# Summing four bilinear corners by one strided VectorE reduce in place of two adds

## The chip, the cores and the metric

One core of a Trainium2 chip. The metric is the device time of one execution in microseconds, the median of several runs.

## The reference

Four images of 128 channels and 56 x 56 pixels, float32. A 1x1 convolution to 32 channels (with batch norm and relu) gives h; a 3x3 convolution of h gives, per pixel, 18 offsets and 9 masks. Then comes a deformable convolution: at each of nine taps h is sampled bilinearly at a shifted position, weighted, and contracted.

```
def gather(yi, xi):
    valid = (yi >= 0) & (yi < Hi) & (xi >= 0) & (xi < Wi)
    ...
    return out * valid[:, None].astype(img.dtype)
return gather(y0, x0) * (wy0 * wx0)[:, None] + gather(y0, x0 + 1) * (wy0 * wx1)[:, None] \
     + gather(y0 + 1, x0) * (wy1 * wx0)[:, None] + gather(y0 + 1, x0 + 1) * (wy1 * wx1)[:, None]
...
samp = _bilinear(h, y, x) * mask[:, None]
out = jnp.einsum('bckhw,ock->bohw', samp, w2.reshape(w2.shape[0], w2.shape[1], 9))
```

A 1x1 convolution back to 128 channels, batch norm, the residual x and relu close the first block. The second is self-attention over the 3136 pixels of an image: f and g of 16 channels give the logits, a softmax over the keys weights h (16 channels), and its projection to 128 channels, times gamma, is added to the input.

## The kernel before

**Front.** For each image TensorE makes h in four shifted copies, VectorE and ScalarE evacuate them, and a table in HBM is written in which one row of 128 floats (512 bytes) holds a pixel's four bilinear corners, 32 channels each. The 27 offset and mask channels go through HBM too.

**Groups and tiles.** The 12544 pixels are taken in 14 groups of 896; a group is 7 tiles of 128 pixels, one pixel per partition (98 tiles). For each group VectorE works out the row indices `IDX` and the corner weights `CW` (`index_step`), two groups ahead in the later part.

**Gathers.** GpSimd (POOL) issues for each tile nine indirect DMAs (L477), one per tap, each fetching a row of 4 x 32 floats per partition into `G[:, j, ...]`, with a memset of a scratch tile `pad` (L484) between two of them. `G` has one slot for each of a group's 7 tiles, so the gathers of tile j of group g wait until VectorE has finished with tile j of group g - 1 (the semaphore `s_s2` before the change). There are 882 gathers and 784 memsets.

**A tile on VectorE.** In a slot the order is tap, corner, channel: 9 x 4 x 32 = 1152 floats. `tile_mul` multiplies them in place by the weights in two instructions (20 and 16 blocks of 32, L1038); `tile_pairs` (L1045) adds corners 0 and 2 to corners 1 and 3 into `S2`, 576 results, both inputs in SBUF; `tile_sum` (L1052) adds the halves of `S2` into `S`, 288 results. TensorE transposes `S` (L578), ScalarE copies it to `ST`, TensorE contracts it with w2 (L586), ScalarE writes `h2`.

**Attention.** A planner (`plan`) writes out a list of ticks for TensorE, VectorE and ScalarE. A tick has a logits block of 112 queries by 448 keys (`logits1`, L602, into PSUM banks L1a and L1b), whose row maximum VectorE takes (`reduce1`, L1060), a second logits block with queries and keys exchanged (L619), its exp on ScalarE (L812), and every fourth tick the product with the values (`weigh`, L633). `l1_free` makes a logits block wait for the reduce two blocks earlier. After a pass over keys come small steps for maxima and sums; `cut` (L1094) splits f and g into bfloat16 parts, with two inputs in SBUF. L1131 and L1174 add the attention and the first block's result to X.

**Order.** `half(g, h, ...)` runs through 28 steps i. HALVES says at which i a tile starts: {3: 0, 7: 1, 13: 2, 19: 3} in the first half, {4: 4, 11: 5, 17: 6} in the second. On VectorE the first product comes at i, the second at i + 1, the pair add at i + 2, the sum at i + 3; TensorE's `tile_in` comes at i + 5. Each step ends with the planned ticks, on all three engines in the same order, 22 to 36 in a half. Groups 0 to 3 run among the fronts of the images. After the last group a half without tiles and the rest of the ticks follow.

Of the kernel before, what the change touches and what calls it, by code (L numbers as in the profile page):

```python
# [27 lines left out]
ALU = mybir.AluOpType  # L28
ACT = mybir.ActivationFunctionType
AX = mybir.AxisListType  # L30

IMAGES, C, HW = 4, 128, 56
CB = 32
# [6 lines left out]
TPG = GROUP // 128  # L40
TAPS = 9
# [27 lines left out]
HALVES = [{3: 0, 7: 1, 13: 2, 19: 3}, {4: 4, 11: 5, 17: 6}]  # L69
# [4 lines left out]
FIN_LAST = dict(w3=0, residual=0, relu=0, project=1, project_in=1, project_g=1, g_in=2, ht_out=3,  # L74
                ht_in=3, cast1=3, cut1=4, cast2=6, cut2=7)
OFFSETS, INDEX, MASKS = 20, 21, 22
TILE_PAIRS, TILE_SUM = 2, 3
TILE_IN, TILE_OUT, TILE_H2 = 5, 7, 7
NEXT = 16
ROWS = 11  # L80
# [151 lines left out]
def build(nc, xt, params, coords, out):  # L232
# [3 lines left out]
    with ExitStack() as ctx:  # L236
        def sb(name, shape, dt=F32):
            return ctx.enter_context(nc.sbuf_tensor(name, shape, dt))
# [4 lines left out]
        def sem(name):  # L243
            return ctx.enter_context(nc.semaphore(name))
# [19 lines left out]
        CW = sb("CW", [128, IRING, TPG, 36])  # L264
        IDX = sb("IDX", [128, IRING, TPG, TAPS], I32)
        G = sb("G", [128, TPG, TAPS * 4 * CB])
        S2 = sb("S2", [128, TAPS, 2 * CB])
        S = sb("S", [128, 2, TAPS * CB])
        ST = sb("ST", [96, 2, 384])
        h2 = sb("h2", [CB, GROUP])  # L270
# [49 lines left out]
        s_it, s_im = sem("s_it"), sem("s_im")  # L320
        s_ie, s_ix = sem("s_ie"), sem("s_ix")
        gathered = [sem(f"gathered{j}") for j in range(TPG)]
        s_mul, s_s2, s_sum = sem("s_mul"), sem("s_s2"), sem("s_sum")
        s_pt, s_st, s_w2 = sem("s_pt"), sem("s_st"), sem("s_w2")
        s_h2 = sem("s_h2")
        s_w3, s_xs, s_x = sem("s_w3"), sem("s_xs"), sem("s_x")
# [33 lines left out]
        def span(h, i):  # L360

            if not FIRST_HALF <= h <= LAST_HALF:
                return range(0)
            lo, n = bound[h], (BLOCKS if h == LAST_HALF else bound[h + 1] - bound[h])
            return range(lo + i * n // BLOCKS, lo + (i + 1) * n // BLOCKS)
# [5 lines left out]
        def after(eng, sem_, count):  # L371


            if not isinstance(count, int) or count > 0:
                eng.wait_ge(sem_, count)
# [88 lines left out]
        @block.gpsimd  # L464
        def _(eng):
            eng.memset(H4[:, :], 0.0).then_inc(s_zero, 1)
            eng.memset(HT[:, :, CI:CI + 1], 1.0).then_inc(s_zero, 1)
            eng.wait_ge(s_zero, 2)
            eng.memset(G6[96:99, :], 1.0).then_inc(s_zero, 1)
            eng.wait_ge(s_zero, 3)  # L470

            def gather(g, images):
                eng.wait_ge(s_ix, NEXT * g + ROWS)
                for j in range(TPG):
                    after(eng, s_s2, TPG * (g - 1) + j + 1)
                    for k in range(TAPS):
                        eng.indirect_dma_start(  # L477
                            G[:, j, k * 4 * CB:(k + 1) * 4 * CB], None,
                            table[0:images * POS, :],
                            bass.IndirectOffsetOnAxis(ap=IDX[:, g % IRING, j, k:k + 1], axis=0))\  # L480
                            .then_inc(gathered[j], 16)
                        if k < TAPS - 1:
                            after(eng, s_pad, (TPG * g + j) * (TAPS - 1) + k)
                            eng.memset(pad[:, :], 0.0).then_inc(s_pad, 1)  # L484

            def tables(n):
                eng.wait_ge(tab_dma[0], 16 * 4 * n)
                eng.wait_ge(tab_dma[1], 16 * 3 * n)

            tables(1)  # L490
            for g in range(3):
                gather(g, 1)
            tables(IMAGES)
            for g in range(3, GROUPS):
                gather(g, IMAGES)
# [434 lines left out]
        def _(eng):  # L930
# [99 lines left out]
            def tile_mul(g, j, first):  # L1030

                eng.wait_ge(gathered[j], 16 * TAPS * (g + 1))
                eng.wait_ge(s_ix, NEXT * (g + 1))
                rows = G[:, j, 0:20 * CB] if first else G[:, j, 20 * CB:]
                n = 20 if first else 16
                weights = CW[:, g % IRING, j, 0:20] if first else CW[:, g % IRING, j, 20:36]
                rows = rows.rearrange("p (k c) -> p k c", c=CB)
                eng.tensor_tensor(rows, rows, weights.unsqueeze(2)  # L1038
                                  .to_broadcast([128, n, CB]), ALU.mult).then_inc(s_mul, 1)

            def tile_pairs(g, j):
                n = TPG * g + j
                eng.wait_ge(s_mul, 2 * (n + 1))
                pair = G[:, j, :].rearrange("p (k a c) -> p k a c", k=TAPS, a=2)
                eng.tensor_tensor(S2[:, :, :], pair[:, :, 0, :], pair[:, :, 1, :], ALU.add)\  # L1045
                   .then_inc(s_s2, 1)

            def tile_sum(g, j):
                n = TPG * g + j
                eng.wait_ge(s_s2, n + 1)  # L1050
                after(eng, s_pt, n - 1 if j else n)
                eng.tensor_tensor(S[:, j % 2, :].rearrange("p (k c) -> p k c", c=CB),  # L1052
                                  S2[:, :, 0:CB], S2[:, :, CB:2 * CB], ALU.add).then_inc(s_sum, 1)

            def reduce1(x):

# [30 lines left out]
            def cut(fin, side, first):  # L1087

                cut_ = P("cut_g" if side else "cut_f", STACK)
                k = 0 if first else 1  # L1090
                to = FG[0:STACK, side, :] if first else \
                    (G6 if side else F6)[0:STACK, bass.ds(fin * CHUNK, CHUNK)]
                eng.wait_ge(s_c1 if first else s_c2, 2 * fin + 1 + side)
                eng.scalar_tensor_tensor(  # L1094
                    out=to, in0=FGh[:, side, :], scalar=cut_[:, k:k + 1],
                    in1=FG[0:STACK, side, :], op0=ALU.mult, op1=ALU.add)\
                    .then_inc(s_d1 if first else s_cut, 1)
# [58 lines left out]
            def half(g, h, fin, idx=None):  # L1156

                at = FIN_LAST if g is None else FIN
                for i in range(BLOCKS):
                    if g is not None and i in HALVES[h]:  # L1160
                        tile_mul(g, HALVES[h][i], True)
                    if g is not None and i - 1 in HALVES[h]:
                        tile_mul(g, HALVES[h][i - 1], False)
                    if g is not None and i - TILE_PAIRS in HALVES[h]:
                        tile_pairs(g, HALVES[h][i - TILE_PAIRS])
                    if g is not None and i - TILE_SUM in HALVES[h]:
                        tile_sum(g, HALVES[h][i - TILE_SUM])
                    for k in range(3 * (i - INDEX), 3 * (i - INDEX) + 3):
                        if idx is not None and 0 <= k < NEXT:
                            index_step(idx, k)  # L1170
                    if fin is not None and i == at["residual"]:
                        eng.wait_ge(s_w3, fin + 1)
                        xc = X[:, fin * CHUNK:(fin + 1) * CHUNK]
                        eng.scalar_tensor_tensor(out=xc, in0=M[:, 0:CHUNK], scalar=scale[:, 2:3],  # L1174
                                                 in1=xc, op0=ALU.mult, op1=ALU.add)\
                            .then_inc(s_xs, 1)
                    if fin is not None and i == at["ht_in"]:
                        eng.wait_ge(s_hT, fin + 1)
                        eng.tensor_copy(HT[:, 4 * fin:4 * fin + 4, 0:CI],
                                        M[0:KT, 0:4 * CI].rearrange("p (k c) -> p k c", c=CI))\  # L1180
                           .then_inc(s_ht, 1)
                    if fin is not None and i in (at["cut1"], at["cut1"] + 1):
                        cut(fin, i - at["cut1"], True)
                    if fin is not None and i in (at["cut2"], at["cut2"] + 1):
                        cut(fin, i - at["cut2"], False)
                    for t in span(LAST_HALF if g is None else 2 * g + h, i):
                        attend(t)
# [22 lines left out]
            front(1)  # L1210
            next_indices(2)
            half(0, 0, None)
            half(0, 1, 0)
            for b in range(2, IMAGES):
                front(b)
                next_indices(b + 1)
                half(b - 1, 0, 2 * b - 3)
                half(b - 1, 1, 2 * b - 2)
# [79 lines left out]
```

## Time and profile before

| | us |
|---|---|
| median of 3 runs | 1559.62 (1557.89 to 1575.72) |
| the profiled execution | 1568.37 |
| its span | 1566.6 |
| POOL busy | 1215.9 (78%) |
| PE (TensorE) busy | 1190.6 (76%) |
| DVE (VectorE) busy | 968.9 (62%) |
| ACT (ScalarE) busy | 681.5 (43%) |
| mean granted TensorE clock | 0.767 of full |

The span runs from the first to the last instruction. Busy time counts instructions in execution; the time in which an engine issues, waits or branches isn't in it. POOL is busy at an even 0.8 from 40 us until 1405 us and idle afterwards, while the others go on. The last gather starts at 1403.9 us.

### The profile page before, as it was taken

The page shows a single profiled execution, that of the slowest core. Times are in us where ns is not written, and L with a number is a line of the kernel's source. Part 1 is how long each engine was busy: PE and PEld are TensorE (multiplying, and loading weights), DVE is VectorE, ACT ScalarE, POOL GpSimd, SP SyncE. Part 2 cuts the span into 40 slices and gives each one's busy share as a digit, 9 for nine tenths or more (in the row PEclk, how much of TensorE's full clock was granted, in tenths as well). Part 3 has the DMA queues.
Part 4 walks back from the last instruction along what each step waited for, and adds up shares of the span by engine and source line. Part 5 has one row for each costly group of instructions (what it writes and reads, how often), then busy time and mean ns, then how long its engine had stood idle before and what let it go on. Part 6 is the DMA issues. An engine that isn't in the chain of part 4 may idle for free.

```text
span 1566.6 us, 18944 instructions
## 1 busy us (share of the span) xinstructions
PE 1190.6 (76%) x5781; PEld 507.6 (32%) x5781; DVE 968.9 (62%) x2171; ACT 681.5 (43%) x1400; POOL 1215.9 (78%) x1673
## 2 busy tenths in 40 slices
PE   5617356388887877898588697898767877889997
PEld 2213122133433333343233242443223323333342
DVE  5444153387866764788466576767655865568781
ACT  2103022143654443465354444546344544457765
POOL 3788888888888888888888888888888888870000
PEclk9756758575978777688777776959577987799998
DMA  3231322211111111121111111121111111110000
GB/s 144 73 120 53 102 75 66 82 42 46 38 42 43 44 50 47 56 66 44 42 43 45 44 50 56 53 58 41 45 40 44 43 50 55 55 51 1 1 12 30
DMA packets 37325, 82.10 MB, mean 52 GB/s; under 512 B 15322, under 2 KB 17486, under 8 KB 36712
## 3 DMA queue, kind: packets, MB, share of 16 engines
q0 software_dynamic: 28224, 57.86, 13.5%
q1 hardware_dynamic: 8964, 22.93, 4.0%
q8 instruction: 47, 0.77, 0.2%
q14 instruction: 54, 0.44, 0.1%
q10 hardware_dynamic: 36, 0.10, 0.0%
HBM read 66.23 MB, written 14.59 MB: 52 GB/s over the span
## 4 chain that ended last, share of the span: by engine, by line
POOL 69%; PE 14%; issue 11%; DVE 5%; DMA 1%; another core or an unknown queue 0%; ACT 0%; POOLq 0%; DVEq 0%
POOL G L477 54%; POOL pad L484 15%; PE PV L633 3%; DVE mxp L1060 2%; PE L1a L602 1%; PE L1b L602 1%; PE L1c L652 1%; PE L1c L669 1%; PE L2a L619 1%; PE L2b L619 1%; DVE fold L1190 1%; DVE G L1038 0%; PE T L586 0%; PE L1c L662 0%
## 5 line engine op out<-in xcount | busy, mean ns | idle before, releaser
L477 POOL DMA_INDIRECT G<-table,IDX x882 | 946.6, 1073 | 187.9 <-issue 158.8
L1060 DVE TENSOR_REDUCE mxp<-L1b 112x1 f32<-112x448 f32 x378 | 234.3, 620 | 143.8 <-PE L1b L602 65.0
L812 ACT ACTIVATE H<-L2b 112x448 f32<-112x448 f32 x370 | 200.5, 542 | 280.1 <-PE L2b L619 187.0
L1060 DVE TENSOR_REDUCE mxp<-L1a 112x1 f32<-112x448 f32 x379 | 234.4, 618 | 69.8 <-PE L1a L602 32.5
L812 ACT ACTIVATE H<-L2a 112x448 f32<-112x448 f32 x370 | 200.1, 541 | 135.0 <-PE L2a L619 93.4
L484 POOL MEMSET pad<- 128x256 f32 x784 | 257.4, 328 | 0.5
L602 PE MATMUL L1b<-G,F 96*112 96x448 bf16 x378 | 174.0, 460 | 88.0 <-DVE mxp L1060 50.6
L633 PE MATMUL PV<-H,HT 112*17 112x448 f32 x1568 | 232.1, 671 | 0.9 <-ACT H L812 0.9
L602 PE MATMUL L1a<-G,F 96*112 96x448 bf16 x379 | 172.1, 454 | 68.9 <-DVE mxp L1060 54.7
L1038 DVE TENSOR_TENSOR G<-G,CW 128x640 f32<-128x640 f32 x196 | 145.8, 750 | 98.2 <-DMA G<-table,IDX 98.2
L619 PE MATMUL L2b<-F,G 99*112 99x448 bf16 x370 | 157.9, 427 | 2.4 <-issue 2.0
L619 PE MATMUL L2a<-F,G 99*112 99x448 bf16 x370 | 157.8, 427 | 2.3 <-issue 1.8
L602 PEld LDWEIGHTS L1b<-G,F 96*112 96x112 bf16 x378 | 55.7, 147 | 252.4 <-DVE mxp L1060 133.5
L586 PE MATMUL T<-ST,par 96*32 96x128 f32 x588 | 107.4, 333 | 8.8 <-ACT ST L798 7.2
L602 PEld LDWEIGHTS L1a<-G,F 96*112 96x112 bf16 x379 | 57.0, 150 | 162.4 <-DVE mxp L1060 80.2
L578 PE MATMUL T<-par,S 128*96 128x128 f32 x294 | 68.5, 357 | 33.2 <-DVE S L1052 23.8
L586 PEld LDWEIGHTS T<-ST,par 96*32 96x32 f32 x588 | 70.1, 132 | 60.1 <-issue 37.0
L798 ACT COPY ST<-T 96x384 f32<-96x384 f32 x98 | 46.3, 473 | 76.4 <-PE T L578 62.7
L803 ACT ACTIVATE h<-T,fold 32x128 f32<-32x128 f32 x98 | 43.9, 448 | 81.3 <-PE T L586 59.1
L1045 DVE TENSOR_TENSOR S<-G 128x576 f32<-128x576 f32 x98 | 73.5, 750 | 0.7
L652 PEld LDWEIGHTS L1c<-par,PVs 128*112 128x112 f32 x432 | 58.2, 210 | 35.3 <-issue 34.1
L619 PEld LDWEIGHTS L2a<-F,G 99*112 99x112 bf16 x370 | 58.0, 157 | 23.8 <-issue 14.8
(124 smaller groups left out, 1314.3 us busy)
## 6 DMA issues: line engine op xcount, KB each, us to landing
G<-table,IDX POOLq DMA_INDIRECT x882
table<-TS SPq DMA_DIRECT2D x24, 256.0 KB
out<-X SPq DMA_DIRECT2D x11, 448.0 KB
X<-xt SPq DMA_DIRECT2D x3, 1568.0 KB, 9.7
out<-X SPq DMA_DIRECT2D x6, 224.0 KB
offd<-OFS SPq DMA_DIRECT2D x28, 47.2 KB
OFG<-offd SPq DMA_DIRECT2D x13, 94.5 KB
X<-xt SPq DMA_DIRECT2D x1, 1120.0 KB, 6.5
```

The costliest lines, as they stand in the source:

```text
L477: eng.indirect_dma_start(G[:, j, k * 4 * CB:(k + 1) * 4 * CB], None, table[0:images * POS, :], bass.IndirectOffsetOnAxis(ap=IDX[:, g % IRI ...
L484: eng.memset(pad[:, :], 0.0).then_inc(s_pad, 1)
L578: mm = eng.transpose(T[0:96, t * 128:(t + 1) * 128], S[:, j % 2, t * 96:(t + 1) * 96], ident)
L586: mm = eng.matmul(O, P("w2", 96)[:, t * CB:(t + 1) * CB], ST[:, j % 2, t * 128:(t + 1) * 128], start=(t == 0), stop=(t == 2))
L602: eng.matmul(l1(x)[0:KT, 0:CHUNK], F6[0:STACK, p.chunk * CHUNK + qt * KT:p.chunk * CHUNK + (qt + 1) * KT], G6[0:STACK, p.image * PIX + kc ...
L619: eng.matmul(l2(y)[0:KT, 0:CHUNK], G6[0:STACK + 3, k:k + KT], F6[0:STACK + 3, p.chunk * CHUNK:(p.chunk + 1) * CHUNK], start=True, stop=Tru ...
L633: mm = eng.matmul(PV[32 * q:32 * q + CI + 1, 0:CHUNK], HT[:, key, :], E[:, y % ERING, :], start=(4 * w == p.block), stop=(4 * w + 4 == p.e ...
L652: mm = eng.matmul(A[0:KT, qt * (CI + 1):(qt + 1) * (CI + 1)], PVs[:, qt * KT:(qt + 1) * KT], P("sel"), start=True, stop=True)
L812: nc.scalar.activation(E[:, y % ERING, :], l2(y)[0:KT, 0:CHUNK], ACT.Exp).then_inc(s_exp, 1)
L1038: eng.tensor_tensor(rows, rows, weights.unsqueeze(2) .to_broadcast([128, n, CB]), ALU.mult).then_inc(s_mul, 1)
L1045: eng.tensor_tensor(S2[:, :, :], pair[:, :, 0, :], pair[:, :, 1, :], ALU.add)\
L1060: eng.tensor_reduce(mxp[:, p.q, qt, kc:kc + 1], l1(x)[0:KT, 0:CHUNK], AX.X, ALU.max)\
```

## The change

The two adds go, and their intermediate `S2`. In their place one `tensor_reduce` reads the slot of `G` as tap, channel, corner, with the corner innermost: 1152 elements, neighbours 32 floats (128 bytes) apart, four of them summed to each of 288 results in `S`. It stands at step i + 2, where the pair add stood, waits for both products, and the gathers wait for it (`s_sum`) in place of the pair add.

```
-TILE_PAIRS, TILE_SUM = 2, 3
+TILE_SUM = 2
-        S2 = sb("S2", [128, TAPS, 2 * CB])
...
-                    after(eng, s_s2, TPG * (g - 1) + j + 1)
+                    after(eng, s_sum, TPG * (g - 1) + j + 1)
...
-            def tile_pairs(g, j):
+            def tile_sum(g, j):
                 n = TPG * g + j
                 eng.wait_ge(s_mul, 2 * (n + 1))
-                pair = G[:, j, :].rearrange("p (k a c) -> p k a c", k=TAPS, a=2)
-                eng.tensor_tensor(S2[:, :, :], pair[:, :, 0, :], pair[:, :, 1, :], ALU.add)\
-                   .then_inc(s_s2, 1)
-
-            def tile_sum(g, j):
-                n = TPG * g + j
-                eng.wait_ge(s_s2, n + 1)
                 after(eng, s_pt, n - 1 if j else n)
-                eng.tensor_tensor(S[:, j % 2, :].rearrange("p (k c) -> p k c", c=CB),
-                                  S2[:, :, 0:CB], S2[:, :, CB:2 * CB], ALU.add).then_inc(s_sum, 1)
+                eng.tensor_reduce(S[:, j % 2, :].rearrange("p (k c) -> p k c", c=CB),
+                                  G[:, j, :].rearrange("p (k a c) -> p k c a", k=TAPS, a=4),
+                                  AX.X, ALU.add).then_inc(s_sum, 1)
...
-                    if g is not None and i - TILE_PAIRS in HALVES[h]:
-                        tile_pairs(g, HALVES[h][i - TILE_PAIRS])
```

## Rows read from the trace of the kernel before

**Rows 1.** The page's chain that ended last: shares by engine, then by line.
```profile
POOL 69%; PE 14%; issue 11%; DVE 5%; DMA 1%; another core or an unknown queue 0%; ACT 0%; POOLq 0%; DVEq 0%
POOL G L477 54%; POOL pad L484 15%; PE PV L633 3%; DVE mxp L1060 2%; PE L1a L602 1%; PE L1b L602 1%; PE L1c L652 1%; PE L1c L669 1%; PE L2a L619 1%; PE L2b L619 1%; DVE fold L1190 1%; DVE G L1038 0%; PE T L586 0%; PE L1c L662 0%
```

**Rows 2.** The chain in order of time: start us, us, what.
```profile
1266.72 2.44 DMA G<-table,IDX
```

**Rows 3.** Waits of POOL: us in total, times, longest us.
```profile
POOL G L477 <- issue: 158.8, 881, 0.3
```

**Rows 4.** Waits of VectorE (DVE), same columns.
```profile
DVE G L1038 <- DMA G<-table,IDX: 98.2, 22, 7.8
```

**Rows 5.** Timeline of VectorE: start us, us, what [idle before, releaser].
```profile
468.93 0.82 DVE L1038 TENSOR_TENSOR G<-G,CW 128x640 f32<-128x640 f32 x1 [3.16 <-DMA G<-table,IDX]
...
1269.18 0.82 DVE L1038 TENSOR_TENSOR G<-G,CW 128x640 f32<-128x640 f32 x1 [5.48 <-DMA G<-table,IDX]
```

**Rows 6.** Waits of TensorE (PE).
```profile
PE L1a L602 <- DVE mxp L1060: 54.7, 42, 7.0
PE L1b L602 <- DVE mxp L1060: 50.6, 31, 6.9
```

**Rows 7.** Busy us of each engine in 885 to 1055 us.
```profile
885.00:1055.00 170.00, 149.55 (x676) 64.16 (x676) 117.51 (x290) 82.87 (x174) 150.31 (x207) 0.72 0.19 54
```
The columns are length, PE, PE weight loads, DVE, ACT, POOL, granted clock, DMA share, GB/s.

**Rows 8.** Groups of VectorE by line and form: busy us, mean ns | idle before.
```profile
L1060 DVE TENSOR_REDUCE mxp<-L1a 112x1 f32<-112x448 f32 x379 | 234.4, 618 | 69.8 <-PE L1a L602 32.5 <-remote 12.7 <-PE L1b L602 12.1
...
L1038 DVE TENSOR_TENSOR G<-G,CW 128x640 f32<-128x640 f32 x98 | 80.2, 819 | 98.2 <-DMA G<-table,IDX 98.2
L1045 DVE TENSOR_TENSOR S<-G 128x576 f32<-128x576 f32 x98 | 73.5, 750 | 0.7
...
L1052 DVE TENSOR_TENSOR S<-S 128x288 f32<-128x288 f32 x98 | 44.3, 452 | 0.5
```

**Rows 9.** Timeline of VectorE at 1423 us: two instructions back to back.
```profile
1423.60 0.75 DVE L1045 TENSOR_TENSOR S<-G 128x576 f32<-128x576 f32 x1
1424.26 0.68 DVE L1094 SCALAR_TENSOR_TENSOR F<-FGh,par,FG 96x448 bf16<-96x448 bf16 x1
```

**Rows 10.** The page's group of the gathers: busy us, mean ns of one.
```profile
L477 POOL DMA_INDIRECT G<-table,IDX x882 | 946.6, 1073 | 187.9 <-issue 158.8
```

**Rows 11.** The line of the gathers: duration ns min/median/max, first and last start.
```profile
L477 POOL DMA_INDIRECT G<-table,IDX x882: 940/950/2721, 43.5 to 1403.9; - x177
```

**Rows 12.** Timeline of POOL: gathers at eight places.
```profile
45.14 0.95 POOL L477 DMA_INDIRECT G<-table,IDX  x1 [0.15 <-issue]
...
109.31 1.10 POOL L477 DMA_INDIRECT G<-table,IDX  x1 [0.17 <-issue]
...
212.62 0.95 POOL L477 DMA_INDIRECT G<-table,IDX  x1 [0.17 <-issue]
...
711.06 1.37 POOL L477 DMA_INDIRECT G<-table,IDX  x1 [0.16 <-issue]
...
712.92 1.41 POOL L477 DMA_INDIRECT G<-table,IDX  x1 [0.16 <-issue]
...
1258.63 1.17 POOL L477 DMA_INDIRECT G<-table,IDX  x1 [0.17 <-issue]
...
1260.30 1.61 POOL L477 DMA_INDIRECT G<-table,IDX  x1 [0.17 <-issue]
...
1397.95 0.95 POOL L477 DMA_INDIRECT G<-table,IDX  x1 [0.17 <-issue]
```

**Rows 13.** Timeline of VectorE from 710.8 to 714 us: the adds.
```profile
710.86 0.75 DVE L1045 TENSOR_TENSOR S<-G 128x576 f32<-128x576 f32 x1
...
713.05 0.45 DVE L1052 TENSOR_TENSOR S<-S 128x288 f32<-128x288 f32 x1
```

**Rows 14.** Timeline of all engines from 309.9 to 322.8 us, two of its rows.
```profile
310.01 0.45 DVE L1052 TENSOR_TENSOR S<-S 128x288 f32<-128x288 f32 x1
...
322.30 0.94 POOL L477 DMA_INDIRECT G<-table,IDX  x1 [0.30 <-issue]
```

More of the change, by code:

```diff
@@ L322, in build @@
         gathered = [sem(f"gathered{j}") for j in range(TPG)]
-        s_mul, s_s2, s_sum = sem("s_mul"), sem("s_s2"), sem("s_sum")
+        s_mul, s_sum = sem("s_mul"), sem("s_sum")
         s_pt, s_st, s_w2 = sem("s_pt"), sem("s_st"), sem("s_w2")
```

## The prediction

> **What bounds the kernel now.** I read the chain of waits first. GpSimd (POOL) has 69% of it, nearly all of it the gathers of L477 (54%) and the memsets between them (15%) [rows 1]. Followed in time, the chain runs through the gathers up to 1266.72 us, where it changes over to the landing of a gather, and from there on it goes through TensorE and VectorE [rows 2]. So there are two stretches: up to 1269 us the gathers set the pace, after that the attention blocks do. The waits say how tightly. The gathers never wait for VectorE to give a slot of `G` back: POOL's idle time is 0.18 us of issue per gather, 158.8 us in 881 pieces, and one wait at the start [rows 3]. VectorE, on the other hand, waits 98.2 us in 22 pieces for gathered rows [rows 4]; the first of them ends at 468.93 us and the last at 1269.18 [rows 5]. TensorE's waits for the maxima (L1060), 54.7 and 50.6 us [rows 6], are about as long together as VectorE's own wait for the gathers: TensorE mostly waits for VectorE while VectorE waits for POOL. In 885 to 1055 us, where VectorE runs behind the gathers, TensorE is busy 149.6 of 170 us and VectorE 117.5 [rows 7]; there VectorE isn't the tighter engine.
>
> **What each part costs.**
>
> *Removed:* 98 times two adds, 750 ns (L1045) and 452 ns (L1052) [rows 8]. Back to back, an instruction starts before the end shown for the one ahead of it: the add at 1423.60 lasts 0.75 us and the next starts at 1424.26, 0.66 us later [rows 9]. So a pair takes about 1.20 - 2 x 0.09 = 1.02 us of VectorE.
>
> *Added:* 98 reduces that read 1152 elements and write 288. No row shows a read whose neighbouring elements lie 32 words apart. The nearest rows: the reduce of L1060, the same operation, reads 448 in 618 ns, and the adds of 576 and 288 elements give a slope of (750 - 452)/288 = 1.035 ns with about 153 ns fixed; 448 x 1.035 + 153 = 617, so the reduce has the adds' price per element read [rows 8]. The floor is 1152 x 1.035 + 153 = 1345 ns, occupying 1.26 us, or +0.24 us a tile. The step could cost more. For the upper end I let each read take two turns: 1152 x 2.07 + 153 = 2538 ns, occupying 2.45 us, or +1.43 us a tile; that is an estimate from the same slope. I take the floor, since L1060 is the same operation and since the add of L1045, which hops every 64 elements on both inputs, keeps the plain slope. The other end stays for the range.
>
> *Where that lies:* until 1269 us VectorE's extra work is covered by its 98.2 us of waits for gathers. After it lie eleven sums, tile 3 of group 12 to tile 6 of group 13: 11 x 0.24 = 2.6 us if all of it is exposed. The cover is one microsecond per tile (98.2/98), so it is gone once a tile costs +1.0 us, which is a reduce of 1.02 + 1.00 + 0.09 = 2.11 us, or 1.70 ns per element.
>
> *What the adds do to the gathers:* this is the larger term. A gather lasts 940 ns at least, 950 at the median, and 1073 on average, up to 2721 [rows 10, 11]: 882 x 0.123 = 108 us of POOL lies above the median. I sorted all 882 by what VectorE runs at the same time. In 480 of them (first at 45.14, last at 1397.95) it runs nothing with two inputs in SBUF, though reduces, reciprocals, copies and L1131, L1174 do run, and these together have no excess over 950 ns: none is above 1.00 us. The excess lies with the two-input instructions: the products (L1038), the cuts (L1094) and these two adds. The gather at 711.06 starts in the add of 710.86 to 711.61 and takes 1.37 us; the one at 712.92 meets the add of 713.05 to 713.50 and takes 1.41, its excess of 0.46 being that add's own length [rows 12, 13]. Not each is hit: that at 212.62 overlaps an add and takes 0.95. Before 1269 us, 81 gathers (212.62 to 1260.30) meet an add and no product or cut, with 28.0 us of excess in all; 56 more (109.31 to 1258.63) meet an add and one of these, with 20.6 us [rows 12]. In these I give the adds a third, since the product or cut is the longer: 6.9 us. The reduce has one input in SBUF, as L1016 and L985 have, which stand among the 480. So the gathers' path to the last wait gets 28.0 + 6.9 = 34.9 us shorter; the bounds are 28.0 and 48.6, and nothing if the products and cuts catch those gathers in the adds' place.
>
> The Trainium skill ("SBUF — State Buffer", Who interferes with whom) has the same split as a rule: a VectorE instruction with two SBUF inputs contends with a GpSimd instruction that reads SBUF, and `tensor_reduce` on trn2 never does. The sum above needs only the 480 and the 81.
>
> *Moved:* the release of a slot of `G` now comes with the sum, at the step where the pair add stood; the sum itself comes one block earlier. The tightest slot shows an add at 310.01 and the gather that reuses it at 322.30 [rows 14], 11.8 us of room, at a time when the gathers are far ahead of VectorE. A pass of 1.3 us fits. Behind the long reduce queue the maxima of L1060, and TensorE's logits behind these; two banks of PSUM let them wait one instruction of that length. One semaphore wait goes, S2 goes, both at nothing: VectorE shows no idle time before these adds. The wait on `s_pt` comes one block earlier, for a tile transposed long before. TensorE's work stays as it is.
>
> **The sum.** -34.9 + 2.6 = -32.3 us. The profiled execution took 1568.4 us (span 1566.6, 1.8 us around it), which gives 1536.1; it lay 8.8 us above the median of the runs, 1559.6, so against the median I expect 1527.
>
> **The rivals.**
>
> *The strided read is dearer, but covered (0.23).* For: the four inputs of a sum lie 128 bytes apart and nothing in the trace reads so. Against: the hops of L1045 cost nothing. Half way between my ends a tile costs +0.84 us: 87 x 0.84 = 73 us of the waits are used, unevenly (30 tiles pass before the first wait [rows 5]), and the eleven last sums put 9.2 us on the end. Between -34.9 + 9.2 = -26 and about -4 when half the gathers' relief meets a VectorE that is behind: 1534 to 1556, say 1545.
> The Trainium skill ("Vector Engine (DVE) Microarchitecture Reference", Measured stream behaviour on trn2) speaks against the change here: runs shorter than two adjacent words slow a port, a source that hops at every element taking 1.73 ns per column. By that figure the reduce would take, as an estimate, 1152 x 1.73 + 153 = 2146 ns, right at the point where the cover ends. The same section has a one-source op, writing one word for two read, that kept the full rate while it hopped. No row here decides.
>
> *VectorE becomes the bound; the slower side (0.11).* Place: the tiles' steps in every group. If a read takes two turns, a tile costs +1.43 us; all exposed, 98 x 1.43 - 98.2 = +42 us: 1602. It decides from 2.11 us per reduce. Against: TensorE was the busier engine behind the gathers [rows 7], so part would be hidden.
>
> *The relief doesn't come (0.16).* The gathers that no longer meet an add meet a product or cut instead, or the stretches where VectorE is behind take it up. For: half of the excess is already theirs. Against: an instruction's chance to be hit goes with its length, and theirs doesn't grow. Then +2.6 us: 1562.
>
> **Chances.** The forecast has 0.50, spread from 1513 (48.6 us of relief) to 1538. Faster by over 2% means below 1528.4: 0.38, 0.35 from the forecast (seven tenths of it) and 0.03 from the first rival with all 48.6 us of relief; slower by over 2%: 0.11; between them 0.51. 2% is about what a measurement can tell here, the three runs being 1.1% apart. The range, 1512 to 1563, leaves out the slow rival and the tails.
>
> **What would show it.** L1045 and L1052 gone and 98 reduces of S from G at 1.35 us (right), about 2.1 (first rival) or 2.5 (second). The gathers' mean at about 1.03 us in place of 1073 ns, the last one starting some 37 us before 1404. The wait of VectorE for gathers near 98 - 24 - 35 = 39 us or somewhat more, no POOL wait for VectorE. Wrong if the gathers' mean stays at 1.07, or if TensorE's wait for L1060 rises while the waits for gathers vanish.

## The result, and the profile after

The changed kernel takes 1521.7 us (median of 4 runs, 1517.9 to 1529.5) beside 1562.3 us for the kernel before: a ratio of 0.9754, 95% interval 0.9713 to 0.9796, or 40.6 us less. The profiled execution took 1523.2 us, its span 1521.3. The forecast was 1527 us against a median of 1559.6. Medians leave out runs that lie more than 1.5% above the fastest of their kernel: below, this changes the one-input twin's, while two kernels whose runs spread further are given by their range.

The page's groups for the gathers, the products and the new reduce (busy us, mean ns | idle before, releaser):

```profile
L476 POOL DMA_INDIRECT G<-table,IDX x882 | 909.9, 1032 | 186.9 <-issue 158.4
L1037 DVE TENSOR_TENSOR G<-G,CW 128x640 f32<-128x640 f32 x196 | 145.7, 750 | 135.1 <-DMA G<-table,IDX 135.0
L1044 DVE TENSOR_REDUCE S<-G 128x288 f32<-128x1152 f32 x98 | 209.7, 2139 | 0.7
```

Two things stand here side by side. The gathers fell from 1073 to 1032 ns [rows 10], 36.7 us over the 882 of them. The reduce takes 2139 ns where the two adds took 750 and 452 [rows 8], so VectorE is busy 92 us longer, and the kernel is faster all the same. The chain of the page still has the same shape as [rows 1]:

```profile
POOL 69%; PE 14%; issue 10%; DVE 5%; DMA 1%; ACT 0%; POOLq 0%; DVEq 0%
POOL G L476 54%; POOL pad L483 15%; PE PV L632 3%; DVE mxp L1053 2%; PE L1b L601 1%; PE L1a L601 1%; PE L1c L651 1%; PE L2a L618 1%; PE L2b L618 1%; DVE S L1044 1%; PE L1c L668 1%; DVE fold L1181 1%; PE T L585 0%; PE T L618 0%; PE L1c L661 0%
```

The waits of VectorE, POOL and TensorE (us in total, times, longest), which answer to [rows 4], [rows 3] and [rows 6]:

```profile
DVE G L1037 <- DMA G<-table,IDX: 135.0, 35, 9.2
...
POOL G L476 <- issue: 158.4, 880, 0.3
...
PE L1a L601 <- DVE mxp L1053: 71.1, 56, 4.1
PE L1b L601 <- DVE mxp L1053: 65.2, 49, 6.4
```

VectorE waits for gathers longer than the profile of before shows, though the gathers are faster and VectorE has more work. TensorE's waits for the maxima, too, are longer than there (136 us in the two rows, 105 before). Both go against the forecast's account, and the second profile of before explains them below. The last such wait comes with the very last tile:

```profile
1368.63 0.83 DVE L1037 TENSOR_TENSOR G<-G,CW 128x640 f32<-128x640 f32 x1 [2.23 <-DMA G<-table,IDX]
...
1371.98 2.17 DVE L1044 TENSOR_REDUCE S<-G 128x288 f32<-128x1152 f32 x1
1374.06 0.68 DVE L1087 SCALAR_TENSOR_TENSOR F<-FGh,par,FG 96x448 bf16<-96x448 bf16 x1
```

So the gathers now set the pace up to the end of their own stage. Last, one gather beside one reduce, in the timelines of VectorE and POOL:

```profile
92.43 2.11 DVE L1044 TENSOR_REDUCE S<-G 128x288 f32<-128x1152 f32 x1
...
93.11 0.95 POOL L476 DMA_INDIRECT G<-table,IDX  x1 [0.17 <-issue]
```

The gather at 93.11 runs wholly inside a reduce and takes 0.95 us, the undisturbed time. There are at least 66 such gathers (93.11 to 1360.44), none above 0.97 us. Of all 882, 159 meet the reduce and nothing with two inputs in SBUF; their excess over 0.95 us is 0.0 us in sum. In the profile of before the 95 that met only an add had 31.7 us.

### The profile page after: what moved, and what is told of

Same layout as the page of the kernel before. It is cut to its first block, busy times and chain, and to the rows that moved or that the text cites. A ratio compares the mean times of both kernels' runs of the same rounds, so it can differ in the third digit from the quotient of the medians.

```text
span 1521.3 us, 18846 instructions
## 1 busy us (share of the span) xinstructions
PE 1191.1 (78%) x5781; PEld 518.1 (34%) x5781; DVE 1062.6 (70%) x2073; ACT 684.6 (45%) x1400; POOL 1179.2 (78%) x1673
## 4 chain that ended last, share of the span: by engine, by line
POOL 69%; PE 14%; issue 10%; DVE 5%; DMA 1%; ACT 0%; POOLq 0%; DVEq 0%
POOL G L476 54%; POOL pad L483 15%; PE PV L632 3%; DVE mxp L1053 2%; PE L1b L601 1%; PE L1a L601 1%; PE L1c L651 1%; PE L2a L618 1%; PE L2b L618 1%; DVE S L1044 1%; PE L1c L668 1%; DVE fold L1181 1%; PE T L585 0%; PE T L618 0%; PE L1c L661 0%
## 5 line engine op out<-in xcount | busy, mean ns | idle before, releaser
L476 POOL DMA_INDIRECT G<-table,IDX x882 | 909.9, 1032 | 186.9 <-issue 158.4
L1053 DVE TENSOR_REDUCE mxp<-L1a 112x1 f32<-112x448 f32 x379 | 233.6, 616 | 50.6 <-PE L1a L601 49.0
L632 PE MATMUL PV<-H,HT 112*17 112x448 f32 x1568 | 240.9, 695 | 0.9 <-ACT H L811 0.9
L1037 DVE TENSOR_TENSOR G<-G,CW 128x640 f32<-128x640 f32 x196 | 145.7, 750 | 135.1 <-DMA G<-table,IDX 135.0
L601 PE MATMUL L1a<-G,F 96*112 96x448 bf16 x379 | 176.8, 466 | 72.2 <-DVE mxp L1053 71.1
L601 PE MATMUL L1b<-G,F 96*112 96x448 bf16 x378 | 177.5, 470 | 67.5 <-DVE mxp L1053 65.2
L1044 DVE TENSOR_REDUCE S<-G 128x288 f32<-128x1152 f32 x98 | 209.7, 2139 | 0.7
L618 PE MATMUL L2a<-F,G 99*112 99x448 bf16 x370 | 162.2, 438 | 0.3 <-ACT H L811 0.3
L585 PE MATMUL T<-ST,par 96*32 96x128 f32 x588 | 111.7, 343 | 7.9 <-ACT ST L797 7.9
L601 PEld LDWEIGHTS L1a<-G,F 96*112 96x112 bf16 x379 | 57.6, 152 | 168.2 <-DVE mxp L1053 108.7
L577 PEld LDWEIGHTS T<-par,S 128*96 128x96 f32 x294 | 42.6, 165 | 108.6 <-issue 81.8
```

What stands on the lines that cost most here:

```text
L476: eng.indirect_dma_start(G[:, j, k * 4 * CB:(k + 1) * 4 * CB], None, table[0:images * POS, :], bass.IndirectOffsetOnAxis(ap=IDX[:, g % IRI ...
L577: mm = eng.transpose(T[0:96, t * 128:(t + 1) * 128], S[:, j % 2, t * 96:(t + 1) * 96], ident)
L585: mm = eng.matmul(O, P("w2", 96)[:, t * CB:(t + 1) * CB], ST[:, j % 2, t * 128:(t + 1) * 128], start=(t == 0), stop=(t == 2))
L601: eng.matmul(l1(x)[0:KT, 0:CHUNK], F6[0:STACK, p.chunk * CHUNK + qt * KT:p.chunk * CHUNK + (qt + 1) * KT], G6[0:STACK, p.image * PIX + kc ...
L618: eng.matmul(l2(y)[0:KT, 0:CHUNK], G6[0:STACK + 3, k:k + KT], F6[0:STACK + 3, p.chunk * CHUNK:(p.chunk + 1) * CHUNK], start=True, stop=Tru ...
L632: mm = eng.matmul(PV[32 * q:32 * q + CI + 1, 0:CHUNK], HT[:, key, :], E[:, y % ERING, :], start=(4 * w == p.block), stop=(4 * w + 4 == p.e ...
```

## The experiments

Twelve runs. Each has the kernel before beside it on the same chip; medians and ratios are to that. "Excess" is the time of the 882 gathers above 0.95 us each, in sum: the group's busy time less 882 x 0.95 = 837.9 us. Each edit is against the changed kernel, but for the second profile of before and the two runs with the adds, which are edits of the kernel before.

**The kernel before once more.** An unused constant, so that every line number is one higher; nothing else.

> The kernel before, unchanged, for a second profile of it. Theory (the adds hold up the gathers, 36 us of the gain): gathers again at 1073 ns on average, 0.95 us where VectorE runs nothing with two inputs in SBUF; time 1562. Open beside it: in the profile of before, TensorE and VectorE show 35 and 76 us of idle time with no releaser (issue, remote) before L602 and L1060, and the profile of after shows none. If that is how this program's records fall in any execution, it is here again; if it was that one execution, it is gone here, and the 9 us by which the profiled gain (45 us) exceeds the relief of the gathers (36 us) belong to that execution.

1559.4 us, ratio 0.9985 (0.9952 to 1.0019). The gathers are as they were (mean 1073 ns, excess 108.2 us beside 108.7), and the 493 that meet nothing with two inputs have none. But the idle time without a releaser is gone, and the wait for gathers is 243.9 us, not 98.2. The first row is of the first profile of before, the second of this one:

```profile
DVE TS L940 <- remote: 49.8, 9, 23.7
```

```profile
DVE G L1039 <- DMA G<-table,IDX: 243.9, 50, 10.6
```

In the first profile VectorE's idle time of this kind (issue and remote, over all its lines) sums to 206 us. It cost no time: up to the end of the last gather VectorE is busy for nearly the same time in both profiles. In the rows below the numbers behind the window are its length and the busy us of TensorE, its weight loads, VectorE, ScalarE and POOL. The first row is of the first profile, the second of this one, the third of the changed kernel:

```profile
0.00:1404.90 1404.90, 1046.95 (x4913) 446.06 (x4913) 864.93 (x1904) 576.78 (x1179) 1215.93 (x1673) 0.75 0.20 57
```

```profile
0.00:1403.70 1403.70, 1054.04 (x4949) 463.40 (x4949) 866.77 (x1912) 582.24 (x1187) 1215.38 (x1673) 0.71 0.20 57
```

```profile
0.00:1367.20 1367.20, 1054.28 (x4982) 460.80 (x4982) 968.69 (x1829) 588.91 (x1198) 1179.16 (x1673) 0.72 0.20 59
```

VectorE is idle 540 and 537 us of this stretch, only under other names. So the waits for gathers that could cover more work were not 98 us but 244. In the changed kernel 398.5 us of idle time are left. The 138 us that are gone are the 36.5 us by which the stretch is shorter and the 102 us by which VectorE is busy longer in it. The waits for gathers gave 109 of them (243.9 to 135.0), other waits of VectorE the rest. TensorE's waits for the maxima, the other row that had looked wrong, are 173 us here and 136 in the changed kernel. The tail beyond the gathers differs from one execution to the next: from the last gather's end to the span's end it is 164 us here (1403.7 to 1568.1) and 154 us in the changed kernel (1367.2 to 1521.3). The granted clock of the last stretch goes with it, 0.85 here and 0.94 there (the column before the last two):

```profile
1430.00:1568.00 138.00, 124.58 (x698) 50.42 (x696) 77.67 (x207) 82.88 (x177) 0.00 (x0) 0.85 0.03 13
```

```profile
1385.00:1521.00 136.00, 121.20 (x730) 50.38 (x730) 81.61 (x216) 87.42 (x187) 0.00 (x0) 0.94 0.03 13
```

The gathers' end moved by 36.5 us (1403.7 to 1367.2); the rest of the 40.6 us between the medians, some 4 us, is no more than these tails vary. What sets the clock there wasn't tried, and that the clock makes the tail's length isn't shown.

**The adds with one more one-input instruction.**

```
+                eng.tensor_reduce(DMY[:, 0:1], par[:, 0:864], AX.X, ALU.max)
                 pair = G[:, j, :].rearrange("p (k a c) -> p k a c", k=TAPS, a=2)
```

> The kernel before with one more VectorE instruction per tile ahead of the pair add: a maximum over 864 elements of par (one input, about 1.05 us), so that VectorE has about the work of the changed kernel and the adds still stand. Its result is not used. Theory (the adds' two inputs hold up the gathers; VectorE's extra work is covered by its waits): gathers stay at 1.07 us on average, the time stays at the kernel before's, 1555 to 1575. Rival 1 (the gain comes from VectorE's later or different timing, not from what the adds read): gathers fall toward 1.03 and the time toward 1525. Rival 2 (VectorE's extra work costs time that the relief hid): 1590 or more.

1547.2 us, ratio 0.9889 (0.9833 to 0.9945): 14 us faster than before, with 102 us more on VectorE (98 x 1043 ns), and 25 us slower than the changed kernel, whose VectorE has about as much to do. The gathers:

```profile
L478 POOL DMA_INDIRECT G<-table,IDX x882 | 936.5, 1062 | 187.4 <-issue 158.7 <-DVE MK L1017 28.8
```

The extra work costs nothing, against rival 2. But 1062 ns isn't 1073: excess 98.6 us in place of 108.2. So about 10 us of relief comes with a shift of when VectorE's instructions run, not from what the adds read. Rival 1 holds for that quarter of the gathers' relief (and for 14 of the 40 us of time). The excess also moves between instructions: gathers that meet an add have 57.6 us of it in the second profile of before and 30.6 here, all the others 50.6 and 68.0. I can't say what in the shift does it.

**A twin: two inputs, or one, ahead of the reduce.** The two probes have the same length, 0.74 us, read the same tile and write a tile nobody reads (576 elements of it with two inputs, one element with one):

```
+                eng.tensor_tensor(DMY[:, :], par[:, 0:576], par[:, 288:864], ALU.add)
```

```
+                eng.tensor_reduce(DMY[:, 0:1], par[:, 0:576], AX.X, ALU.max)
```

> The changed kernel with one tensor_tensor of 576 elements per tile ahead of the reduce, both inputs from par in SBUF, 0.75 us, its result unused. Theory: the gathers it meets are held up as by the pair add: mean from 1032 back to about 1055 to 1065 ns, last gather 20 to 28 us later than in the changed kernel, time 1542 to 1552. Rival (what VectorE reads doesn't matter): mean stays at 1032, time 1522 to 1530.

> The twin of the two-input probe: a maximum over the same 576 elements of par, one input, also about 0.75 us, result unused. Theory: gathers stay at 1.03 us on average, time 1521 to 1530, the difference being only the tail after the last wait. Rival (any VectorE work of that length slows the gathers or uses up the cover): as slow as its two-input twin.

Two inputs: 1571.2 us, ratio 1.0043 (1.0010 to 1.0075). One input: 1543.1 us, ratio 0.9875 (0.9833 to 0.9916). Their gathers, in that order:

```profile
L477 POOL DMA_INDIRECT G<-table,IDX x882 | 946.0, 1073 | 186.5 <-issue 158.7 <-DVE MK L1016 27.9
```

```profile
L477 POOL DMA_INDIRECT G<-table,IDX x882 | 912.9, 1035 | 187.3 <-issue 158.4 <-DVE MK L1016 28.6 <-DVE S L1046 0.3
```

This is the cleanest evidence for the relief: the same length and place of VectorE work, and the probe with two SBUF inputs costs 33 us of gathers (excess 108.1 and 75.0; last gather's end 1402.9 and 1370.4) and 28 us of time. In the one-input twin 207 gathers meet the reduce or the probe and nothing with two inputs, with no excess.

The two probes also differ in what they write. Writing isn't what holds a gather up: in the profile of before 23 gathers meet the copy of L940, which reads PSUM and writes 512 elements of SBUF, and nothing with two inputs, and none of them takes over 0.95 us. Nor do two inputs when one of them lies in PSUM: 33 gathers meet L1131 or L1174 in this way, and none takes over 0.98 us. One copy, and the gather that starts inside it:

```profile
261.56 0.69 DVE L940 COPY TS<-L2a 128x512 f32<-128x512 f32 x1
```

```profile
261.74 0.95 POOL L477 DMA_INDIRECT G<-table,IDX  x1 [0.17 <-issue]
```

Both times came out over what I expected, by 19 to 29 us and 13 to 22 us. The one-input twin's profile (an execution of 1555.5 us, 12 above its median) shows where: its gathers end 3 us after those of the changed kernel, but its last sum comes 35 us after the last gather (7 us in the changed kernel). The waits for gathers fell to 74.7 us, the last at 1142 us, and from there on VectorE and TensorE are behind. The cover ends between +1.0 and +1.7 us a tile, and gradually.

**The reduce made twice.** The first writes a tile nobody reads.

```
+                eng.tensor_reduce(DMY[:, :].rearrange("p (k c) -> p k c", c=CB),
+                                  G[:, j, :].rearrange("p (k a c) -> p k c a", k=TAPS, a=4),
+                                  AX.X, ALU.add)
```

> The changed kernel with the strided reduce made twice (the first into a tile that nobody reads), so that VectorE has 2.05 us more per tile and nothing with two inputs more. Theory: that is beyond the cover (135 us of waits for gathers in all, 88 us of them after 440 us, where 68 tiles come): 68 x 2.05 - 88 = 51 us and more, as the one-input probe of 0.66 us per tile already cost 25: 1575 to 1610, with hardly a wait for gathers left, gathers still at 1.03 us. Rival (TensorE hides it): under 1560.

1655.1 us, ratio 1.0605 (1.0569 to 1.0640). The gathers are at 1027 ns, so they aren't to blame:

```profile
DVE G L1038 <- DMA G<-table,IDX: 13.9, 3, 7.1
...
POOL G L477 <- DVE S L1048: 41.2, 9, 11.9
```

POOL now waits for VectorE, and the page's chain runs mostly through TensorE and VectorE:

```profile
PE 45%; DVE 37%; POOL 10%; issue 7%; DMA 1%; ACT 0%; DVEq 0%; POOLq 0%; ACTq 0%
```

This is the slower rival's mechanism. It is dearer than I expected: two thirds of the 201 us added come through.

**Corners innermost.** The table's rows are written as channel, corner; products and reduce run over neighbours. Same output.

```
-                eng.tensor_copy(TS[:, i % 2, 0:n], L2[i % 2][:, 0:n]).then_inc(s_tev, 1)
+                eng.tensor_copy(TS[:, i % 2, 0:n].rearrange("p (j c a) -> p j c a", c=CB, a=4),
+                                L2[i % 2][:, 0:n].rearrange("p (j a c) -> p j c a", c=CB, a=4))\
+                   .then_inc(s_tev, 1)
...
-                n = 20 if first else 16
+                n = 5 if first else 4
...
+                rows = rows.rearrange("p (k c a) -> p k c a", c=CB, a=4)
+                weights = weights.rearrange("p (k a) -> p k a", a=4).unsqueeze(2)
...
-                                  G[:, j, :].rearrange("p (k a c) -> p k c a", k=TAPS, a=4),
+                                  G[:, j, :].rearrange("p (k c a) -> p k c a", k=TAPS, a=4),
```

> The changed kernel with the table's rows written as channel, corner in place of corner, channel (by the evacuation copy that fills TS), so that the products and the reduce run over contiguous elements; same output. Theory: the dear reduce (2139 ns, 1.73 ns per element) is the price of the step of 32 floats; contiguous it takes 1.35 us. It was covered anyway: VectorE's waits for gathers grow by some 50 to 75 us, gathers stay at 1.03 us, the last tile still waits for its gather, so the time falls only by what the last tile's chain gets shorter, 0.8 us, and by lag here and there: 1512 to 1522. Rival (VectorE's length counts throughout): 98 x 0.79 = 77 us less, 1445.

1521.0 us, ratio 0.9721 (0.9696 to 0.9746), as good as the changed kernel's 1521.7.

```profile
L1047 DVE TENSOR_REDUCE S<-G 128x288 f32<-128x1152 f32 x98 | 131.7, 1344 | 0.7
...
L1040 DVE TENSOR_TENSOR G<-G,CW 128x640 f32<-128x640 f32 x98 | 80.6, 823 | 193.2 <-DMA G<-table,IDX 193.1
```

The same reduce over contiguous elements takes 1344 ns. The step of 32 floats is 0.80 us of the 2139 ns, 78 us over the kernel, and taking it away gains no time: 58 of the 78 us went into the wait for gathers (135 to 193 us), the rest into other waits of VectorE.

**Without the memsets between the gathers,** with the reduce and with the adds. The memsets produce nothing that is read.

```
-                        if k < TAPS - 1:
-                            after(eng, s_pad, (TPG * g + j) * (TAPS - 1) + k)
-                            eng.memset(pad[:, :], 0.0).then_inc(s_pad, 1)
```

> The changed kernel without the 784 memsets between the gathers. Theory (the gathers set the pace): POOL needs 0.33 us and some issue less per gather; if a gather's own time stays at 1.03 us the last one ends some 250 us earlier, and VectorE and TensorE become the bound: 1400 to 1470. Rival (the memsets hide something, such as a queue that makes the next gather wait): gathers grow to about 1.3 us and the time stays within 10 us of the changed kernel's.

> The kernel before without the memsets, the twin of the one above. Theory: where POOL is no longer the bound, the adds' relief is worth nothing and the reduce's 1.03 us more of VectorE per tile count: this one is faster than the changed kernel without memsets, by 30 to 90 us if POOL really stops being the bound. If the time is still set by the gathers, the changed kernel keeps its lead.

Reduce: 1400.2 us (1396.4 to 1410.4), ratio 0.8973. Adds: 1387.7 us (1385.1 to 1388.9), ratio 0.8877. The order is turned round: with the last gather some 150 to 170 us earlier, the change loses 12.6 us. Gathers and waits of the two, the reduce first:

```profile
L476 POOL DMA_INDIRECT G<-table,IDX x882 | 907.5, 1029 | 296.9 <-issue 267.6 <-DVE MK L1012 28.4 <-DVE S L1041 0.9
...
DVE G L1034 <- DMA G<-table,IDX: 17.5, 7, 6.7
```

```profile
L477 POOL DMA_INDIRECT G<-table,IDX x882 | 923.0, 1046 | 297.7 <-issue 267.4 <-DVE MK L1013 29.1 <-DVE S L1042 1.2
...
DVE G L1035 <- DMA G<-table,IDX: 112.2, 30, 8.2
```

The relief is there (last gather's end 1219 and 1235 us), but VectorE no longer has the waits to pay for the reduce. The loss is smaller than the 30 to 90 us expected.

**Contiguous reduce, no memsets.**

> Contiguous reduce (1344 ns) and no memsets; same output. Theory: without memsets the adds gave 1388 with gathers at 1046 ns, the strided reduce 1400 with gathers at 1029 ns and VectorE's waits for them down to 17 us; the contiguous reduce has the relief and costs only +0.24 us of VectorE per tile over the adds, so the last gather ends near 1219 and most of the 16 us lead over the adds' gathers (1235) shows: 1366 to 1382, the fastest of all. Rival (without memsets VectorE's length counts whatever the gathers do): 1388 to 1400.

**The sum one block later.**

```
-TILE_SUM = 2
+TILE_SUM = 3
```

> The changed kernel with the reduce at step i + 3, where the second add stood, in place of i + 2; everything else equal. Theory (its place is no part of the gain): gathers at 1.03 us on average, 1517 to 1530. Rival (part of the gain comes from the sum being ready one block earlier): 1535 or more.

These two ran in one job and came out at 1946.6 to 1981.1 us and 1614.8 to 1652.2 us, far outside every expectation. Their gathers were not slow (1002 and 1027 ns). Their profiles have the idle time without a releaser in all three engines; VectorE's waits in the first:

```profile
DVE mxp L1053 <- remote: 301.0, 67, 17.0
...
DVE H L945 <- remote: 116.6, 8, 37.7
```

I ran both kernels again, word for word.

> The kernel with the reduce one block later, word for word, once more. It took 1649 us and its profile has idle time of TensorE, VectorE and ScalarE with no releaser, as the first profile of before has and as the second of before, the changed kernel and six other probes have not. If that idle time belongs to the conditions of the job and not to the program (the gathers were at 1.03 us as expected), it is gone here and the time is 1517 to 1530. If it belongs to the program, the time is 1615 to 1652 again, and the place of the sum matters.

> The contiguous reduce without memsets, word for word, once more. It took 1968 us, with some 500 us of such idle time. Conditions of the job: 1366 to 1388 here, beside 1388 of the adds without memsets. The program: 1946 to 1981 again.

The sum one block later: 1525.1 us, ratio 0.9739 (0.9673 to 0.9804), gathers at 1031 ns; its place is no part of the gain. The contiguous reduce without memsets: 1366.8 us (1365.3 to 1377.1), ratio 0.8748 (0.8682 to 0.8815), the fastest kernel of the study, 21 us below the adds without memsets. The idle time without a releaser is gone in both. Its rows:

```profile
L476 POOL DMA_INDIRECT G<-table,IDX x882 | 897.3, 1017 | 296.1 <-issue 268.2 <-DVE MK L1014 27.6 <-DVE S L1044 0.3
...
L1044 DVE TENSOR_REDUCE S<-G 128x288 f32<-128x1152 f32 x98 | 131.5, 1342 | 0.7
```

## Why the prediction was right, and where not

The time fell where the forecast had it (1521.7 us, in its spread of 1513 to 1538), and the mechanism, relief of the gathers, is shown. Two other terms were wrong, and that they cancelled is luck. More than 2% faster had been given 0.38, less than "between".

*The gathers set the pace:* right, and more than the first profile let one see. The two stretches I saw, before and after 1269 us, were those of an execution with idle time that has no releaser. In the second profile of before, VectorE's last wait for a gather ends at 1364.92 us.

*The relief of the gathers:* right. 34.9 us forecast up to the last wait, 36.7 us measured on POOL over all gathers, and the twins show the cause: 33 us between a probe with two SBUF inputs and one with one. The assumption behind it, that products and cuts don't take the adds' place, held in sum: 72.0 us of excess are left, all beside two-input instructions. Of before's 108.7 us, 77 remain when the 31.7 of the gathers that met only adds are taken off. About 22 of the 77 lay in gathers that met an add together with a product or cut; some 5 of these went too, where a third, 7, had been assumed. Whether single gathers moved onto products and cuts can't be told from sums, and part of the relief, about 10 us as the adds with an extra one-input instruction show, hangs on timing. The prediction puts all excess on products, cuts and adds. The small two-input instructions of `index_step` and of the maxima hold gathers up as well, but little: 95 gathers meet only such, with 2.2 us.

*The price of the reduce:* wrong. I took the floor, 1345 ns, because the same operation had the adds' slope on contiguous elements and because L1045 hops and keeps that slope; the strided reduce takes 2139 ns. The floor is right for a contiguous read (1344 ns). L1045 was no guide: by its access pattern it adds corners 0 and 1 to corners 2 and 3, in runs of 64 adjacent floats, while the reduce never reads two neighbours in a row. The first rival's condition came true, with its cost per tile: +0.84 us assumed, and (2.14 - 0.09) - 1.02 = +1.03 measured. The figure of the Trainium skill that stood beside it ("Vector Engine (DVE) Microarchitecture Reference", Measured stream behaviour on trn2: 1.73 ns per column for a source that hops at every element) gives 2146 ns as an estimate, and the trace agrees at 2139, though the table's hop is 4 KiB and the step here is 128 bytes. The same section's case of a hopping source at full rate is not what this reduce shows.

*The cover:* wrong in the other direction. I read 98.2 us of waits for gathers, one microsecond a tile, and put the end of the cover at a reduce of 2.11 us. By this a reduce of 2.14 us would have eaten the gain: 98 us of waits less 101 for the work and 35 for the earlier gathers is -38. The cover was 243.9 us. The error was to take the named wait as the whole slack in a profile that had 206 us of VectorE's idle time under "issue" and "remote", most of it time that belonged to the same slack. The two errors cancelled: 98 x 0.79 = 78 us more work than forecast met 146 us more cover. With the cover that I had read, the price of the reduce would have undone the forecast.

*The sum:* -32.3 us forecast, -40.6 measured. The tail term of +2.6 us isn't visible: the last sum ends 7 us after the last gather, and 13 and 21 us after it in the two profiles of before.

*The slower rival:* its mechanism exists, and its point lies further out. An added 1.03 us a tile costs nothing that shows (1521.7 us, beside 1521.0 with the contiguous reduce at +0.24), 1.7 us costs 21 us, 3.1 us costs 133 us. With the memsets gone the point moves in, and the change is a loss of 12.6 us.

*The relief doesn't come:* not so; the gathers' mean fell to 1032 ns.

## What to carry to other kernels

Before pricing an edit on one engine, look at what its instructions do to the queue that sets the pace: here the saving came from GpSimd's gathers, and VectorE itself got more to do. Sort the pacing engine's instructions by what runs beside them; a mean above the median (1073 beside 950 ns) says that something holds some of them up. Slack can stand under other names than the wait for the pace setter, or under none, so count all idle time of the covered engine; a second profile of the same kernel is the cheapest check of it.

An edit that trades time on a covered engine for relief on the bound one holds only while that bound stands. Once it is lifted, the trade must be made cheap as well: the contiguous layout was worth nothing at first and 33 us (1400 to 1367) without the memsets.

## What the runs showed of the hardware

- A gather that meets a VectorE instruction with two inputs in SBUF can be held up (up to 1.11 us beyond 0.95 where it met only an add, in the second profile of before). Beside one-input instructions none of hundreds was, at least 66 of them lying wholly inside a reduce, nor beside instructions whose second input lies in PSUM. The Trainium skill ("SBUF — State Buffer", Who interferes with whom) has it so. The memsets of POOL, which read nothing, take 328 or 329 ns on average in every profile that has them.
- A reduce of 1152 float32 elements takes 2139 ns at a step of 32 floats and 1344 ns at a step of one, in the same grouping by four. The grouping costs nothing beside the slope of the adds, which gives 1345.
- The same program can run with idle time that no record explains: 1615 to 1652 and then 1525 us, 1947 to 1981 and then 1367 us. In the job with the long times the kernel before still took 1566.6 us; its own slack of 244 us may well hide such idle time, as it did in its first profile. What makes it stays open. In such a stretch TensorE's last record ends some microseconds before the instructions of VectorE and ScalarE that wait for it start; no instruction load took longer than in the other runs.
